# 28 transpositions of the identity on TensorE ahead of the first modulation columns

## What is computed

```python
mod = (_silu(L0_c) @ L0_wmod).reshape(L0_c.shape[0], 6, 1, -1)   # (4,512) @ (512,3072)
sa, ca, ga, sb, cb, gb = (mod[:, 0], mod[:, 1], mod[:, 2], mod[:, 3], mod[:, 4], mod[:, 5])
h = _layernorm(x, axis=-1) * (1 + ca) + sa
x = x + ga * attn(h)     # causal 4-tap conv, B/C/delta products, a scan over the sequence, out product
h = _layernorm(x, axis=-1) * (1 + cb) + sb
x = x + gb * ffn(h)      # router picks one of 2 experts; 512 -> 2048 -> 512
```

## Time and profile before

| what | us |
|---|---|
| median of 3 runs | 607.64 |
| lowest and highest | 602.56, 609.18 |
| the profiled execution, its time | 607.99 |
| its span | 606.3 |

### The profile page before, as it was taken

The page is one execution under the profiler, slowest core; times in us unless marked ns, Lnnn a source line. Parts: engine busy times, 40 slices in busy tenths (PEclk is TensorE's granted clock), DMA queues, the critical chain, the costliest instruction groups (busy, mean ns, idle before and its releaser), DMA issues.

```text
span 606.3 us, 8147 instructions
## 1 busy us (share of the span) xinstructions
PE 533.0 (88%) x2419; PEld 426.7 (70%) x2419; DVE 344.3 (57%) x752; ACT 263.9 (44%) x519; POOL 137.7 (23%) x140
## 2 busy tenths in 40 slices
PE   4999999779743699999999999999999999997970
PEld 4957666346522688888888888988978888885760
DVE  3257967959877775436535544544544544533790
ACT  2426254583865564334434434443443434430320
POOL 1000002103020312211311311312303113177474
PEclk9997978969876799999999999999999999997995
DMA  8903321041040202202202102021020120047596
GB/s 307 388 0 113 89 98 51 0 140 58 13 140 1 72 4 72 71 1 70 68 4 71 38 38 70 3 70 44 28 72 7 65 71 1 2 121 188 66 119 81
DMA packets 15067, 44.23 MB, mean 73 GB/s; under 512 B 5040, under 2 KB 5088, under 8 KB 11680
## 3 DMA queue, kind: packets, MB, share of 16 engines
q1 hardware_dynamic: 10656, 34.69, 16.9%
q0 software_dynamic: 4352, 8.69, 8.1%
HBM read 34.93 MB, written 8.71 MB: 72 GB/s over the span
## 4 chain that ended last, share of the span: by engine, by line
PE 79%; DVE 7%; ACT 6%; issue 3%; DMA 1%; POOL 1%; ACTq 1%; DVEq 1%; SPq 0%; POOLq 0%
PE bank L904 31%; PE bank L930 30%; PE bank L728 4%; PE bank L763 2%; ACT XSfull L604 2%; PE bank L803 2%; PE bank L756 2%; PE bank L784 2%; PE bank L807 2%; PE bank L769 2%; DVE xc L1031 1%; ACT XSfull L608 1%; DMA wm<-wmod 1%; POOL out L507 1%; ACT z L525 1%
## 5 line engine op out<-in xcount | busy, mean ns | idle before, releaser
L465 POOL TENSOR_TENSOR Wlo<-raw,Whi x56 | 71.1, 1291 | 257.9 <-ACT Whi L691 257.9
L904 PE MATMUL bank<-XShi,Whi 128*128 x320 | 115.6, 361 | 14.3 <-ACT XShi L667 12.6
L1345 DVE TENSOR_TENSOR acc<-acc,bank 128x512 f32<-128x512 f32 x119 | 80.9, 687 | 66.1 <-PE bank L930 57.4
L904 PE MATMUL bank<-XShi,Wlo 128*128 x320 | 115.1, 360 | 0.0
L904 PE MATMUL bank<-XSlo,Whi 128*128 x320 | 115.0, 359 | 0.0
L930 PE MATMUL bank<-Whi,ahi 128*128 128x512 f32 x272 | 107.1, 394 | 6.7 <-issue 5.0
L1329 DVE TENSOR_TENSOR twice_h<-twice_h,bank 128x512 f32<-128x512 f32 (+2 forms) x80 | 48.3, 607 | 111.0 <-ACT twice_h L676 108.9
L930 PE MATMUL bank<-Wlo,ahi 128*128 128x512 f32 x272 | 107.0, 393 | 0.0
L930 PE MATMUL bank<-Whi,alo 128*128 128x512 f32 x272 | 106.8, 393 | 0.1
L685 ACT ACTIVATE ahi<-twice_h 128x512 fp32r<-128x512 f32 (+2 forms) x80 | 45.4, 567 | 123.0 <-PE bank L930 115.3
L676 ACT ACTIVATE twice_h<-bank 128x512 f32<-128x512 f32 (+2 forms) x80 | 42.4, 532 | 100.4 <-PE bank L904 91.7
(11 more groups left out here) (157 smaller groups left out, 584.6 us busy)
## 6 DMA issues: line engine op xcount, KB each, us to landing
raw<-wffn SPq DMA_DIRECT2D x16, 1024.0 KB, 5.2
wm<-wmod SPq DMA_DIRECT2D x6, 1024.0 KB, 13.4
x_in<-x SPq DMA_DIRECT2D x4, 1024.0 KB, 9.1
out<-res SPq DMA_DIRECT2D x4, 1024.0 KB, 5.0
ga_bc<-ga_rows SPq DMA_DIRECT2D x4, 256.0 KB, 3.5
bc<-router_rows SPq DMA_DIRECT2D x4, 256.0 KB, 3.6
wx_sb<-wx SPq DMA_DIRECT2D x1, 514.0 KB, 8.3
gb_row<-gb_rows,sorted_meta POOLq DMA_INDIRECT x17
```

What stands on the lines that cost most here:

```text
L465: pool.tensor_tensor(Wlo[:, hb % 2, c, :], raw[:, c, :], Whi[:, hb % 2, c, :].bitcast(F32), ALU.subtract).then_inc(s_wlo, 1)
L904: mm = pe.matmul(hP[(par + u) % 2][m][:, c0:c1], W[wp][:, par, 2 * e + k // 2, o:o + P], XS[xp][:, k, bass.ds(start_row[u] + c0, c1 - c0)] ...
L1345: dve.tensor_tensor(acc[:, n, :], acc[:, n, :], yP[s][:, :], ALU.add).then_inc(s_yu, 1)
```

## The change

TensorE waits for GpSimd's constants first, then transposes the identity 28 times into the four quarters of bank pX, and then goes on as before. The results in pX are not read; the state product overwrites them later. No other engine's program is touched.

```diff
+WARM = 28
...
+            pe.wait_ge(s_const, 9)
+            for n in range(WARM):
+                pe.transpose(pX[:, P * (n % 4):P * (n % 4) + P], ident[:, :], ident[:, :])
             pe.wait_ge(s_silu, 1)
             mod_columns(0)
             mod_columns(1)
-            pe.wait_ge(s_const, 9)
             transposes1(0)
```

## The result

The changed kernel took 618.36 us (median of 4 runs, 617.82 to 619.34), where the kernel before has a median of 605.25 us in 4 runs (602.56 to 609.18). The ratio is 1.0213, with a 95% interval of 1.0143 to 1.0284: slower by 1.4 to 2.8%, where I had forecast a small gain. Medians and counts here are of all runs, ratios and their intervals of those within 1.5% of their kernel's fastest. The profiled execution took 618.18 us, against 607.99 us before, 10.2 us more. It is these 10.2 us that the profiles can account for. The medians are 13.1 us apart, because two of the four runs before were near 602.7 us and the profiled one was not.

The account below looks back on a forecast made before the run. TensorE was taken to carry the early chain, at the low clock to about 38.4 us. 607.99 - 2.0 (early clock) + 0 (later stretches) = 606.0 us, less 0.35 to the median, rounded to 605.5; range 600.5 to 609.0.

Parts of the forecast that it names:

- The early clock: Start of TensorE's work: transpositions from 2.5 us raise the clock at 5.3 to 7.9 us, speeding line 728's column products.
- the term of 2.0 us: First column products, line 728: 2.1 us at the high clock level, saving 0.97 us each, 2.0 us saved.
- the ends of 0 and 3.5: Line 728: limits of the saving, 0 if the clock is lost in the rest, 3.5 us if raised late and held.
- Rival A: Line 728: transpositions don't raise the clock or it is lost before 8.7 us; products keep 13.8 us, 607.7 us; chance 0.17.
- The moved wait and the fit: TensorE's start: the moved constants wait costs nothing; 28 transpositions fit before the weights at 8.57 us, cost 0 to 0.1 us.
- What happens to it later: Low-clock stretches after 32.99 us: eight may each move 1.3 us either way; sum taken as 0, spread 1.8 us.
- Rival B: Lines 763 and 769: the earlier start misses the clock rise, 4.3 us more, net +2.3, 609.9 us; chance 0.10.
- What the change adds: TensorE's start: 28 transpositions (28 loads, 28 products) and the moved wait, nothing removed; nothing waits for pX; no DMA touched.
- rival C: Code cut elsewhere: another stall like that at 551.29 us costs 7.1 us, 612.7 us, chance 0.05; its going gives 598.5, 0.04.

## Why the prediction was wrong

- **The early clock** was right in mechanism. The rise came at about 8.0 us (forecast 5.3 to 7.9), the transpositions ended at 8.43 us (forecast 7.3 to 8.3), line 728's products took 11.47 us (forecast 10.5 to 13), and the term of 2.0 us measured 2.31 us in the changed kernel's profile. In the other five profiles with the transpositions it was between 0.7 us (transpositions as a loop) and 3.1 us, inside the ends of 0 and 3.5; so that this profile came so near to 2.0 us is partly luck. Rival A falls with it.
The page on TensorE which says that transposing doesn't engage the full clock (the Trainium skill, TensorE: Matmul & The Clock Gate, Part 4: PE-mode transpose) is contradicted here: the clock rose after transpositions alone, by 8.0 us in all six profiles that have them at the start, and column products in their place did not raise it.
- **The moved wait and the fit** were right: the column products began 0.11 us later, and the weights came as much later, at 8.68 instead of 8.57 us.
- **What happens to it later** was taken as 0 with 1.8 us of spread. Measured: 1.5 us more lead up to the state product, then 2.7 us of it lost, of which 1.5 us in the skip products that ran at the low level, and 1.04 us left at the loop. The net, 1.2 us lost, lies within what I gave.
- **Rival B** did not occur: line 763's eight took 5.81 us and line 769's 3.44 us.
- **The step that failed** is in "What the change adds", where the cost of the added instructions was counted as their time at the start, and their place in memory was left to rival C with 0.05. In its place the runs showed two turns of the expert loop, each 5.7 us longer (3.49+2.23 and 4.15+1.56 us), and the same stalls with no transposition at all. Rival C had the mechanism's name, and the price of one such stall nearly right (7.1 us), but the wrong place. I had read the stall at 551.29 us as code. It is there, between the same two products, in all thirteen profiles at quite different positions of the code: the two begin 4.6 to 4.8 us apart in eleven of them, 4.1 and 5.3 us in the other two, and before the change no piece was fetched during it. So nothing ties it to the position of the code, and its own cause is open. The rows that mattered were the small ones at the turns, 0.93 and 0.62 us, which have no place in my argument: they mark where the loop goes back to its head, and a piece is fetched about 1.9 us after they begin. How long TensorE then stands depends on how many products the head holds ahead of the next piece. What the small stall itself is, no run shows: before the change no piece was fetched during it.
- So the sum is -2.3 (early clock) +1.3 (later stretches, and the 0.11 us) +11.4 (two turns) = +10.4 us where I had -2.0. The unlikeliest rival decided, at a chance of 0.05, because I gave the shift of the code no look of its own: 55 instructions are a fifth of a piece, so a stall that depends on a border within 55 instructions of the present place had a fair chance, an estimate from this one count.

## What to carry to other kernels

Instructions added in front of a long loop (here 2378 instructions) are not free where their time is hidden: they shift the loop, and each turn may then stand until the next piece of code is there. Before such a change look at the small "issue" stalls at the loop's turns and at how many products the head's first piece holds, and test a change in front of a loop beside a version with the same shift and no work. With the shift made harmless, the warm-up was measured three times: 0.9962 (0.9916 to 1.0008), 0.9950 (0.9908 to 0.9992) and 0.9934 (0.9883 to 0.9984) of the time before, a gain of about half a per cent that is hardly clear of the noise. Medians of all runs give 0.9944 to 0.9959.

## What the hardware showed that I had not expected

The second stall in the head, by how many of its products lie ahead of the border:

| the loop moved by | products ahead of the border | stall behind them, us (turn 1, turn 2) | products behind it |
|---|---|---|---|
| 12 | 12 | 0.80, 0.63 | high level |
| 24 | 6 | 1.78, 2.32 | high level |
| 37 | 1 | 3.07, 3.35 | low level at first |
| 55 (waits only) | 0 | 4.27, 4.78, in one with the first | low level at first |

Each product (0.25 us in this place) ahead of the border takes about its own time off the stall: from 12 products to 6 it grows by 1.3 us, from 6 to 1 by 1.2 us (means of the two turns). Counted from the turn's beginning, the product behind the border starts at nearly the same time whatever lies ahead of it: after 4.27, 4.34, 4.30 and 4.27 us at the first turn of the four runs, 4.42 us in the changed kernel, and after 4.45 to 4.78 us at the second. That is what one fetch, asked for at the turn, would give. Before the change some 17 products and the first stall take about 5.2 us (an estimate from 17 x 0.25 + 0.93), so nothing is left to wait for.

The clock falls during or right behind the long stalls, which adds 1.4 to 2.2 us to the 24 products; behind the stalls of up to 2.3 us it adds nothing.

By the starts of the transpositions, the rise came at about 5.3, 5.8, 6.2, 6.3, 7.1 and 8.0 us in the six profiles. The best case for the columns was not the latest rise, as I had argued, but the two earliest: those kept the high level to 12.2 and 12.6 us, the two near 6.2 us lost it at 9.7 us.

The third thing is the spread. In three profiles of one kernel, the one with 28 transpositions and the loop moved by 257, the expert products began at 192.71, 197.33 and 201.70 us. In the kernel with columns in place of the transpositions they began at 202.51 us. Of the 9.8 us between this and the earliest, the first 3.1 us are the early clock; the rest came later, some of it from bursts that met a rise or missed it (the third set took 3.72 against 6.62 us). The kernel before shows runs near 602.5 and near 608 us, few between.
